# Self attention's group loop written out and folded, its scales made by a power on GpSimd, and the mixture's selector product moved behind the up product

## The chip, the cores and the metric

The kernel runs on one core of one Trainium2 chip. A core has five engines with a queue of their own each: TensorE (PE in the profile), VectorE (DVE), ScalarE (ACT), GpSimd (POOL) and SyncE (SP, which here only issues DMAs). An engine works its queue strictly in order; engines meet through semaphores alone. The metric is the device time of one execution in microseconds; lower is better.

## The reference, cut to what matters

The input `x` has 16 batch elements of 128 tokens with 128 features, the context 16 times 77 tokens. Four steps are added to `x`, each with a gate `tanh(g)` in front and a layer norm of `x` as its input:

```
x = x + tanh(g_xattn[0]) * strided_attention(layernorm(x), ctx, ctx)   # stage A: 16 heads, head h sees keys h, h+16, h+32, h+48
x = x + tanh(g_ffn[0])   * block(layernorm(x))                         # stage B: full self attention, then a mixture of 8 experts + shared
x = x + tanh(g_xattn[1]) * similarity_attention(layernorm(x), ctx)     # stage C, inside the mixtures
x = x + tanh(g_ffn[1])   * mixture(layernorm(x))                       # 16 experts + shared
```

Stage A, for one batch element: `Q = xn Wq^T + bq`, `K = ctx Wk^T + bk`, `V = ctx Wv^T + bv`, scores of each head over its 4 keys divided by sqrt(8), softmax over the 4, times `V`, then `Wo` and `bo`. Stage B begins with a layer norm followed by an RMS norm, and both need the mean and the variance of every row of `x` after stage A.

## The kernel before

The work is written out by hand for each engine in `build`; the order of the calls is the order of each queue, and there is no planner.

Stage A works through 4 groups of 4 batch elements. On DVE `norm` (line 757) makes the normalised tokens of a group, PE turns them over (`turn_and_project`, line 1235), ACT copies them out of PSUM (line 509), and PE multiplies them with Wq (line 1239, 512 columns) and the context with Wk and Wv (lines 1241 and 1242, 256 columns each). DVE adds the biases and masks keys and values by head (lines 786 and 789), PE multiplies the values by Wo (line 1248), and DVE adds `bo` (line 799). `strided_scores` (line 1256), DVE's maximum and subtraction (806, 808), ACT's exponential (513), DVE's sum, reciprocal and product (813 to 815), `turn_probabilities` (1263), ACT's copy (516), `attend` (1273), and DVE's update of `X` with new row statistics (`attended`, lines 823 and 827) close the group. Groups 0 to 2 run in a hardware loop (`Fori`) of all three engines, with one buffer of each kind; PE passes the next group's projections between scores and probabilities of this one. GpSimd has no part in the loop.

After group 3, DVE computes in a chain of single small instructions the moments of all 16 batch elements and the two inverse square roots (lines 744 to 861; a shift of bits as first guess and three Newton steps). Only then may GpSimd begin stage B.

Stage B goes batch element by batch element. GpSimd's `slot` makes in turn: the splitting of keys (lines 399 to 401), the normalised input `Z` of a later element (394), the splitting of queries (406 to 409), and `halves_of_weights` (420, 421), two pieces of the first mixture's weights. PE turns keys and queries over (line 1334), and works scores, values and denominators (1301 to 1328). All of it is staggered over slots: PE's `slot(of)` works on six elements at once.

Then follow the router and, from 218 us on, the two mixtures with stage C spread among them, in 112 chunks of 512 tokens (`chunks`). In a chunk PE makes the gate product in three passes (lines 1453 to 1455), at the first chunk of an expert the selector product `bc` (line 1498), which spreads the tokens' weights of this expert over all partitions into one PSUM bank, then the up product, then the down product of the chunk three before. ACT makes the silu (632) and a rounded copy (625), DVE multiplies silu by `bc` (1062) and by up (1067), and GpSimd subtracts the rounded copy (461).

## Time and profile before

| what | value |
|---|---|
| median of 3 runs | 563.38 us (563.04 to 566.1) |
| the profiled execution | 563.62 us, its span 561.9 us |
| mean granted TensorE clock | 0.929 of full speed |
| busy in the span | PE 467.4, DVE 403.4, ACT 265.8, POOL 257.3 us |
| first `Z` of stage B on GpSimd | at 66.97 us |
| first chunk of the mixtures on PE | at 218.00 us |

Times are microseconds from the start of the span; "ns" is said where meant. "PE L1453" is a matmul of line 1453. In a view of one stretch, `[1.59 <-DVE work L1062]` says that the engine had been idle for 1.59 us just before this instruction, and what its wait ended with. `x4` is the number of instructions in a row. One float32 matmul of the program appears as two in the trace. What lies outside the span, 1.7 us in the profiled execution, belongs to its time.

### The profile page before, as it was taken

The page shows a single profiled execution, that of the slowest core. Times are in us where ns is not written, and L with a number is a line of the kernel's source. Part 1 is how long each engine was busy: PE and PEld are TensorE (multiplying, and loading weights), DVE is VectorE, ACT ScalarE, POOL GpSimd, SP SyncE. Part 2 cuts the span into 40 slices and gives each one's busy share as a digit, 9 for nine tenths or more (in the row PEclk, how much of TensorE's full clock was granted, in tenths as well). Part 3 has the DMA queues.
Part 4 walks back from the last instruction along what each step waited for, and adds up shares of the span by engine and source line. Part 5 has one row for each costly group of instructions (what it writes and reads, how often), then busy time and mean ns, then how long its engine had stood idle before and what let it go on. Part 6 is the DMA issues. An engine that isn't in the chain of part 4 may idle for free.

```text
span 561.9 us, 10894 instructions
## 1 busy us (share of the span) xinstructions
PE 467.4 (83%) x3679; PEld 349.4 (62%) x3679; DVE 403.4 (72%) x1051; ACT 265.8 (47%) x494; POOL 257.3 (46%) x363
## 2 busy tenths in 40 slices
PE   2576279999999466999979988999798989798896
PEld 2344147676667354777757776768576766576674
DVE  6567568888987644895775677777877787677763
ACT  0211057777776234655536533644355346443452
POOL 6000079988960030555554544345445444343453
PEclk9878589999999855999989997999899999998999
DMA  6500000201010000200000000000000000000000
GB/s 163 173 0 0 0 3 2 85 23 51 3 34 19 1 0 0 48 0 1 1 2 0 2 1 2 1 0 0 0 0 1 0 1 1 20 0 21 0 20 19
DMA packets 19325, 9.79 MB, mean 17 GB/s; under 512 B 6508, under 2 KB 18765, under 8 KB 19277
## 3 DMA queue, kind: packets, MB, share of 16 engines
q1 hardware_dynamic: 16829, 8.77, 5.5%
q10 hardware_dynamic: 2448, 0.40, 0.4%
q8 instruction: 27, 0.44, 0.4%
q14 instruction: 21, 0.17, 0.1%
HBM read 8.12 MB, written 1.05 MB: 16 GB/s over the span
## 4 chain that ended last, share of the span: by engine, by line
PE 60%; DVE 18%; issue 8%; POOL 5%; ACT 5%; ACTq 2%; DVEq 1%; POOLq 0%
PE PS L1453 11%; PE PS L1455 10%; PE PS L1454 10%; DVE work L1062 3%; PE PS L1334 3%; PE PS L1323 3%; PE PS L1498 3%; PE PS L1328 2%; PE PS L1368 2%; PE PS L1301 2%; PE PS L1417 2%; PE PS L1239 1%; PE PS L1312 1%; DVE t_b L736 1%; POOL W0L_gate L421 1%
## 5 line engine op out<-in xcount | busy, mean ns | idle before, releaser
L461 POOL TENSOR_TENSOR HLO<-work,HHI 128x512 fp32r<-128x512 f32 x112 | 145.1, 1296 | 185.9 <-ACT HHI L625 185.4
L632 ACT ACTIVATE work<-PS 128x512 f32<-128x512 f32 x112 | 66.8, 597 | 110.1 <-PE PS L1455 106.3
L1062 DVE TENSOR_TENSOR work<-work,PS 128x512 f32<-128x512 f32 x104 | 71.0, 683 | 55.1 <-ACT work L632 53.5
L625 ACT ACTIVATE HHI<-work 128x512 fp32r<-128x512 f32 x111 | 69.5, 626 | 40.2 <-DVE work L1067 40.1
L1067 DVE TENSOR_TENSOR work<-PS,work 128x512 f32<-128x512 f32 x112 | 77.1, 691 | 12.1 <-PE PS L1455 3.4
L1498 PE MATMUL PS<-CWT,sel 128*128 128x512 bf16 (+1 forms) x68 | 27.2, 400 | 24.0 <-DVE work L1062 24.0
L870 DVE TENSOR_REDUCE nmax<-PS 128x4 f32<-128x512 f32 x64 | 42.2, 682 | 6.4 <-PE PS L1301 6.2
L531 ACT ACTIVATE EX<-PS 128x512 f32<-128x512 f32 x64 | 35.2, 605 | 13.3 <-PE PS L1312 13.2
L1453 PE MATMUL PS<-H2H,W0H_up 128*128 128x512 f32 (+1 forms) x72 | 36.8, 512 | 2.9 <-DVE work L1067 2.9
L1453 PE MATMUL PS<-H2H,W0H_gate 128*128 128x512 f32 (+1 forms) x72 | 32.7, 454 | 2.2 <-issue 1.5
L1498 PEld LDWEIGHTS PS<-CWT,sel 128*128 128x128 bf16 x68 | 6.6, 97 | 44.8 <-DVE work L1062 30.0
L394 POOL TENSOR_SCALAR Z<-X,rs,nmr 128x128 f32<-128x128 f32 x16 | 7.2, 449 | 56.1 <-DVE nmr L859 56.1
L1455 PE MATMUL PS<-H2H,W0L_up 128*128 128x512 f32 (+1 forms) x72 | 29.7, 413 | 0.0
L1454 PE MATMUL PS<-H2L,W0H_up 128*128 128x512 f32 (+1 forms) x72 | 29.7, 412 | 0.0
L1454 PE MATMUL PS<-H2L,W0H_gate 128*128 128x512 f32 (+1 forms) x72 | 29.4, 408 | 0.0
L1455 PE MATMUL PS<-H2H,W0L_gate 128*128 128x512 f32 (+1 forms) x72 | 29.3, 407 | 0.0
L1453 PE MATMUL PS<-HHI,W0H_down 128*128 128x512 f32 x72 | 29.2, 405 | 0.0
L1455 PE MATMUL PS<-HHI,W0L_down 128*128 128x512 f32 x72 | 29.1, 405 | 0.0
L1454 PE MATMUL PS<-HLO,W0H_down 128*128 128x512 f32 x72 | 29.1, 404 | 0.0
L549 ACT ACTIVATE QM<-PS 128x1024 bf16<-128x1024 bf16 x16 | 16.4, 1023 | 13.6 <-PE PS L1334 13.6
L1453 PE MATMUL PS<-H2H,W1H_up 128*128 128x512 f32 x40 | 22.5, 561 | 0.0
L1301 PE MATMUL PS<-KT,QT 64*128 64x128 bf16 x256 | 19.6, 218 | 1.7 <-DVE nmax L870 1.1
(290 smaller groups left out, 1174.7 us busy)
## 6 DMA issues: line engine op xcount, KB each, us to landing
X<-in_x_dram SPq DMA_DIRECT2D x4, 256.0 KB, 8.1
raw<-in_L_ffn_e_gate_dram SPq DMA_DIRECT2D x1, 1024.0 KB, 5.4
raw<-in_L_ffn_e_up_dram SPq DMA_DIRECT2D x1, 1024.0 KB, 7.7
out_dram<-X SPq DMA_DIRECT2D x4, 256.0 KB, 2.3
ctx_nat<-in_ctx_dram SPq DMA_DIRECT2D x1, 616.0 KB
raw<-in_L_ffn_We_gate_dram SPq DMA_DIRECT2D x1, 512.0 KB, 4.0
raw<-in_L_ffn_We_up_dram SPq DMA_DIRECT2D x1, 512.0 KB, 3.9
raw<-in_L_ffn_We_down_dram SPq DMA_DIRECT2D x1, 512.0 KB, 4.1
```

Source lines behind the costliest of these rows:

```text
L461: pool.tensor_tensor(HLO[t][:], HH[k % 2][:], HHI[t][:].bitcast(F32), ALU.subtract).then_inc(m_sem["lo"], 1)
L531: act.activation(EX[j][:], PS[:, 2 + j % 2, :], ACT.Exp, scale=SCALE).then_inc(b_sem["exp"], 1)
L625: act.activation(HHI[turn_of(m, g, k)][:], HH[k % 2][:], ACT.Copy).then_inc(S["hi"], 1)
L632: act.activation(SG[c % 2][:], PS[:, c % 2, :], ACT.Silu).then_inc(S["silu"], 1)
L870: dve.tensor_reduce(by_group[:, 4 * (j // 2):4 * (j // 2) + 4, j % 2], PS[:, j % 2, :].rearrange("p (h t) -> p h t", h=4), AX.X, ALU.max, ...
L1062: dve.tensor_tensor(SG[c % 2][:], SG[c % 2][:], PS[:, 4, :], ALU.mult).then_inc(S["scaled"], 1)
L1067: dve.tensor_tensor(HH[c % 2][:], PS[:, 2 + c % 2, :], SG[c % 2][:], ALU.mult).then_inc(S["hid"], 1)
L1301: ins = pe.matmul(PS[:, j % 2, i * P:(i + 1) * P], QT[b % 2][of_head, h // 2, :], KT[b % NKT][of_head, h // 2, :], start=True, stop=True)
L1453: pe.matmul(PS[:, bank, :], high, x_high, start=start, stop=False)
L1454: pe.matmul(PS[:, bank, :], high, x_low, start=False, stop=False)
L1455: return pe.matmul(PS[:, bank, :], low, x_high, start=False, stop=stop)
L1498: pe.matmul(PS[:, 4, :], SEL[m][:, e, :], CWT[:, bass.ds(g * GT, GT)], start=True, stop=True).then_inc(S["bc"], 1)
```

## The change

Stage A:

- The loop is written out for the four groups, and most buffers are doubled: normalised tokens (`XGA`), their transpose (`XGTA`), probabilities (`PA`, `PAT`), keys and values (`KA4`, `VA4`, in the memory of stage B's `QT` and `QM`).
- The query projection goes. Wq is multiplied into the masked keys (`fold_keys`: `KQ = Wq^T K`, 256 columns a group) and the scores are `xn KQ`; the bias bq enters through one more product with a broadcast tile `BQ` (`strided_scores`).
- GpSimd makes the normalised tokens (`normalised_group`) and adds `tanh(g) * bo` to `X` (`bias_group`). ACT, not DVE, copies the folded keys and values out of PSUM.
- GpSimd also makes the scales: of groups 1 to 3 of the first norm (`first_scales`), and of stage B's norms in two halves of 8 batch elements (`scales_of_half`), by an elementwise power -0.5 and one Newton step. DVE keeps the scales of group 0.
- The last group's end is put among stage B's first slots: on DVE `probabilities(3)` and `attended(3)`, on PE `turn_probabilities(3)` and `attend(3)`, on ACT the copies between them.
- Seven small transfers move from ACT's queue to SP's, ahead of stage B's weights; the context comes in two halves, each with a semaphore.

Mixtures: on PE the selector product stands behind the up product. In a chunk the wait for DVE's `scaled` of the chunk before stands there too.

```diff
@@ stage A's tiles
+            XGA, XGTA = [XG, HG1], [XGT, work[0]]
+            KA4, VA4 = ([t[u][:]... for u in range(2)] for t in (QT, QM))
+            KQ = [EX[g][:, 0:GB * NK].rearrange("p (b k) -> p b k", b=GB) for g in range(G)]
@@ GpSimd
+            def moments(at, n):
+                st = stats[:, at, :]
+                pool.tensor_tensor(p_a[:, 0:n], st[:, :, 1], st[:, :, 4], ALU.add)
...
+                step(pool.tensor_tensor(var[:, at], p_b[:, 0:n], p_c[:, 0:n], ALU.add))
+            def inverse_root(y, v, t):
+                step(pool.tensor_tensor(y, v, less_half[:].broadcast_to([P, v.shape[1]]), ALU.pow))
+                step(pool.tensor_tensor(t, y, y, ALU.mult))
+                step(pool.tensor_tensor(t, t, v, ALU.mult))
+                step(pool.tensor_scalar(t, t, -0.5, 1.5, ALU.mult, ALU.add))
+                step(pool.tensor_tensor(y, y, t, ALU.mult))
+            def scales_of_half(k):
+                pool.wait_ge(a_sem["st"], 2 * k + 2)
+                moments(at, HALF)
...
+            normalised_group(0)
+            pool.tensor_copy(BQ[:], bq_c[:].broadcast_to([P, P])).then_inc(a_sem["bq"], 1)
+            first_scales(1, G)
+            normalised_group(1)
...
-            batches(slot, 0, 3)
+            scales_of_half(0)
+            batches(slot, -3, 1)
+            scales_of_half(1)
+            batches(slot, 1, B)
@@ DVE
-            with dve.Fori(0, G - 1) as g:
-                norm(g + 1)
-                less_row_maximum(g)
-                probabilities(g)
-                queries_keys_values(g + 1)
-                attended(g)
-                values_out(g + 1)
...
+            masked_keys_values(0)
+            masked_keys_values(1)
+            less_row_maximum(0)
+            masked_keys_values(2)
+            probabilities(0)
+            less_row_maximum(1)
+            masked_keys_values(3)
+            attended(0)
+            probabilities(1)
+            less_row_maximum(2)
+            attended(1)
+            probabilities(2)
+            less_row_maximum(3)
+            attended(2)
@@ DVE, start of stage B
-            batches(slot, 0, 6)
+            queries_and_keys(0)
+            values_apart(0)
+            probabilities(3)
+            queries_and_keys(1)
+            values_apart(1)
+            turned_keys(0)
+            attended(3)
+            queries_and_keys(2)
+            batches(slot, -3, -1)
...
@@ PE, mixtures
                     split_product(c % 2, WH[m][0][:, c, :], WL[m][0][:, c, :], xh, xl).then_inc(S["g"], 1)
+                    if not (start and c < 2):
+                        pe.wait_ge(S["hid"], base + c)
+                    split_product(2 + c % 2, WH[m][1][:, c, :], WL[m][1][:, c, :], xh, xl).then_inc(S["u"], 1)
                     if first_of_expert(m, c):
                         e = c // per
                         pe.wait_ge(S["scaled"], g * NSC[m] + OFF[m][1] + e * per + 1)
                         pe.matmul(PS[:, 4, :], SEL[m][:, e, :], CWT[:, bass.ds(g * GT, GT)], start=True, stop=True).then_inc(S["bc"], 1)
-                    if not (start and c < 2):
-                        pe.wait_ge(S["hid"], base + c)
-                    split_product(2 + c % 2, WH[m][1][:, c, :], WL[m][1][:, c, :], xh, xl).then_inc(S["u"], 1)
```

PE in stage A, before: the body of the loop, for one group (`ctx_t` is the turned context, `VA` the masked values, `PA` the probabilities).

```order
L1256 MATMUL PS<-KA,work 128x64 x4
L1232 REGISTER_ALU
L1235 MATMUL PS<-identf,XG 128x128 x4
L1239 MATMUL PS<-XGT,w_t 128x512
L1241 ISA
L1241 MATMUL PS<-ctx_t,w_t 128x256
L1242 MATMUL PS<-ctx_t,w_t 128x256
L1263 MATMUL PS<-identf,PA 128x128 x2
L1273 MATMUL PS<-work 128x128 x4
L1248 MATMUL PS<-w_t,VA 128x128 x2
```

PE now, from the scores of group 1 on (`QT` holds the masked keys, `QM` the masked values, `EX` the folded keys, `E3T` the folded values).

```order
L1368 MATMUL PS<-QT,BQ 128x256
L1370 MATMUL PS<-EX,work 128x64 x4
L1343 MATMUL PS<-QT,w_nat 128x256
L1336 MATMUL PS<-ctx_t,w_t 128x256
L1337 MATMUL PS<-ctx_t,w_t 128x256
L1348 MATMUL PS<-w_t,QM 128x128 x2
L1379 MATMUL PS<-identf,work 128x128 x2
L1393 MATMUL PS<-E3T,work 128x128 x4
L1357 MATMUL PS<-identf,XG 128x128 x4
```

The 512 columns of the query projection are gone; 256 columns of the fold and 256 of the bias stand for them, and the context's products of group 3 come before group 0 is closed.

GpSimd at the start of stage B, before: from the last of its constants on.

```order
L361 MEMSET bm 4x1
L394 TENSOR_SCALAR Z<-X,rs,nmr 128x128 x2
L399 TENSOR_TENSOR T<-T,KS 128x128
L400 CAST KS<-T 128x32x8
L401 TENSOR_TENSOR KS<-T,KS 128x16x8
```

GpSimd now, second place: the end of the last weight piece of element 0, and the first rows of the second half's scales (18 instructions; the same 18 stand ahead of the first `Z`, too).

```order
L513 TENSOR_TENSOR W0L_gate<-raw0,W0H_gate 128x256
L385 TENSOR_TENSOR p_a<-stats 128x8
L386 TENSOR_TENSOR p_b<-stats 128x8
L387 TENSOR_TENSOR p_c<-stats 128x8
L388 TENSOR_SCALAR mean<-p_a 128x8
L389 TENSOR_SCALAR p_c<-p_c 128x8
L390 TENSOR_TENSOR p_b<-p_b 128x8
L391 TENSOR_SCALAR p_b<-p_b 128x8
```

Work of DVE has moved to GpSimd, into the row of its slots between elements 0 and 1.

## Rows read from the trace of the kernel before

**Rows 1.** Busy time in stretches: span, PE, PEld, DVE, ACT, POOL, clock, DMA

```profile
30.00:50.00 20.00, 13.55 (x65) 8.94 (x64) 14.07 (x38) 2.57 (x6) 0.00 (x0) 0.84 0.00 0
...
105.00:172.00 67.00, 66.60 (x1237) 46.77 (x1238) 58.31 (x129) 49.68 (x88) 54.16 (x123) 1.00 0.16 44
218.00:562.00 344.00, 308.87 (x1467) 236.80 (x1467) 247.99 (x587) 166.96 (x319) 158.58 (x132) 0.97 0.02 6
```

**Rows 2.** The chain that ended last, in stage A: start us, us, what

```profile
36.50 0.68 PE PS L1235 x4
37.28 0.61 ACT XGT L509
37.93 1.82 PE PS L1239 x2
39.75 0.85 PE PS L1241 x2
...
42.38 0.74 PE PS L1273 x8
...
46.66 0.68 PE PS L1235 x4
```

**Rows 3.** Timeline of the start, all engines: start us, us, instruction, idle before

```profile
8.97 2.26 PE L1226 MATMUL PS<-identf,ctx_nat 77*128 77x77 f32 x16
...
11.22 2.67 DVE L766 BATCH_NORM_STATS2 stats<-X 128x6 f32<-128x128 f32 x12
11.30 0.46 ACTq L495 DMA_DIRECT2D bqv_r<-in_L_xattn_b_qv_dram  x1
...
12.81 1.28 ACT L499 ACT_TABLE_LOAD   x1 [12.81 <-issue]
```

**Rows 4.** DVE's groups of instructions in 35.3 to 45.5: busy, mean ns

```profile
L827 DVE BATCH_NORM_STATS2 stats<-X x4 | 0.9, 282 | 0.1
L786 DVE TENSOR_SCALAR work<-PS,bq_c 128x512 f32<-128x512 f32 x1 | 0.8, 750 | 1.7 <-PE PS L1242 1.7
L813 DVE TENSOR_REDUCE mxA<-PA 128x64 f32<-128x256 f32 x1 | 0.6, 583 | 1.0 <-ACT PA L513 1.0
L814 DVE RECIPROCAL mxA<-mxA 128x64 f32<-128x64 f32 x1 | 0.6, 553 | 0.0
L789 DVE SCALAR_TENSOR_TENSOR KA<-PS,bk_c,hmask 128x256 f32<-128x256 f32 x1 | 0.5, 475 | 0.0
...
L815 DVE TENSOR_TENSOR PA<-PA,mxA 128x256 f32<-128x256 f32 x1 | 0.4, 424 | 0.0
```

**Rows 5.** Timeline at the end of stage A

```profile
62.73 0.18 DVE L744 TENSOR_TENSOR t_a<-stats 128x16 f32<-128x16 f32 x1
...
66.97 0.88 POOL L394 TENSOR_SCALAR Z<-X,rs,nmr 128x128 f32<-128x128 f32 x2 [56.14 <-DVE nmr L859]
```

**Rows 6.** GpSimd's groups by shape, 66 to 172

```profile
L394 POOL TENSOR_SCALAR Z<-X,rs,nmr 128x128 f32<-128x128 f32 x16 | 7.2, 449 | 56.1 <-DVE nmr L859 56.1
...
L369 POOL CAST iota_e<-iota_i 128x16 f32<-128x16 int32 x1 | 0.2, 196 | 0.1
```

**Rows 7.** The page's group of GpSimd's widest operation

```profile
L461 POOL TENSOR_TENSOR HLO<-work,HHI 128x512 fp32r<-128x512 f32 x112 | 145.1, 1296 | 185.9 <-ACT HHI L625 185.4
```

**Rows 8.** The chain that ended last, in stage B

```profile
81.14 0.40 POOL T L399
...
105.33 0.62 PE PS L1334 x8
```

**Rows 9.** Who waited for whom in 200 to 540: total us, times, longest

```profile
PE PS L1498 <- DVE work L1062: 24.0, 11, 4.0
```

**Rows 10.** Timeline of the mixtures, one undisturbed chunk, then the first stall

```profile
228.64 0.39 PE L1498 MATMUL PS<-CWT,sel 128*128 128x512 bf16 x1
...
229.47 0.69 DVE L1062 TENSOR_TENSOR work<-work,PS 128x512 f32<-128x512 f32 x1
...
284.54 0.61 PE L1498 MATMUL PS<-CWT,sel 128*128 128x512 bf16 x1 [3.56 <-DVE work L1062]
```

More of the change, by code:

```diff
@@ L263, in batches @@
         def batches(slot_of, first, last):
-            for s in range(-last, B - first):
+            for s in range(first, last):
                 slot_of(lambda k: s + k if 0 <= s + k < B else None)
@@ L276, in _, with tokens, context @@
         def _(sp):
[L278 removed]
+            def tokens(g):
                 sp.dma_start(X[:, g * GB:(g + 1) * GB, :], a["x"][g * GB:(g + 1) * GB].rearrange("b s d -> s b d")).then_inc(x_in[g], 16)
[L280 to L281 removed]
+            def context(k):
+                at = slice(k * B // 2, (k + 1) * B // 2)
+                sp.dma_start(ctx_nat[:, at, :], a["ctx_1024"][at].rearrange("b s d -> s b d")).then_inc(ctx_in[k], 16)
+            tokens(0)
+            context(0)
+            context(1)
+            for g in range(1, G):
+                tokens(g)
+            smalls = [(n1w[:], col(a["L0_ffn_norm1_w"])), (n2w[:], col(a["L0_ffn_norm2_w"])),
+                      (w1_c[:], col(a["L1_xattn_w_sim"][0:D])), (w2s[:], col(a["L1_xattn_w_sim"][D:2 * D])),
+                      (w3s[:], col(a["L1_xattn_w_sim"][2 * D:3 * D])), (bsim_c[:], row(a["L1_xattn_b_sim"], P)),
+                      (bqv_r[:], row(a["L1_xattn_b_qv"], P))]
+            for to, what in smalls:
+                sp.dma_start(to, what).then_inc(small_in, 16)
             for i, n in enumerate(("wq", "wk")):
@@ new lines, in normalised_group, with bias_group @@
+            def normalised_group(g):
+                if g == 0:
+                    pool.wait_ge(a_sem["ln"], 1)
+                if g >= 2:
+                    pool.wait_ge(a_sem["t"], g - 1)
+                for j in range(GB):
+                    b = g * GB + j
+                    ins = pool.tensor_scalar(XGA[g % 2][:, j, :], X[:, b, :], rstd[:, b:b + 1], nmr[:, b:b + 1], ALU.mult, ALU.add)
+                ins.then_inc(a_sem["xn"], 1)
+            def bias_group(g):
+                pool.wait_ge(a_sem["xn"], g + 1)
+                Xg = X[:, g * GB:(g + 1) * GB, :]
+                pool.tensor_tensor(Xg, Xg, tgbo[:].unsqueeze(1).broadcast_to([P, GB, D]), ALU.add).then_inc(a_sem["bias"], 1)
@@ new lines, in _ @@
+            normalised_group(0)
+            pool.wait_ge(bias_in, 16 * 3)
+            pool.tensor_copy(BQ[:], bq_c[:].broadcast_to([P, P])).then_inc(a_sem["bq"], 1)
+            first_scales(1, G)
+            normalised_group(1)
+            pool.wait_ge(tg_ready, 1)
+            pool.wait_ge(bo_in, 16)
+            step(pool.tensor_scalar(tgbo[:], bo_r[:], tg[:, 0:1], None, ALU.mult))
+            bias_group(0)
+            bias_group(1)
+            for g in range(2, G):
+                normalised_group(g)
+                bias_group(g)
@@ new lines, in masked_keys_values @@
+            def masked_keys_values(g):
+                if g == 0:
+                    dve.wait_ge(bias_in, 16 * 3)
+                    dve.wait_ge(consts, 1)
+                dve.wait_ge(a_sem["kv"], g + 1)
+                if g >= 2:
+                    dve.wait_ge(a_sem["s"], g - 1)
+                    dve.wait_ge(a_sem["v2"], g - 1)
+                mask = hmask[:].unsqueeze(1).broadcast_to([P, GB * L, H])
+                for to, off, bias in ((KA4[g % 2], 0, bk_c), (VA4[g % 2], GB * NK, bv_c)):
+                    ins = dve.scalar_tensor_tensor(
+                        out=to.rearrange("p b (l h) -> p (b l) h", h=H),
+                        in0=PS[:, 5 + g % 2, off:off + GB * NK].rearrange("p (a h) -> p a h", h=H),
+                        scalar=bias[:], in1=mask, op0=ALU.add, op1=ALU.mult)
+                ins.then_inc(a_sem["kv_sb"], 1)
@@ L826, in attended @@
+            def attended(g):
+                dve.wait_ge(a_sem["y"], g + 1)
+                dve.wait_ge(a_sem["bias"], g + 1)
+                Xg = X[:, g * GB:(g + 1) * GB, :]
+                dve.scalar_tensor_tensor(out=Xg, in0=PS[:, 1, :].rearrange("p (b d) -> p b d", b=GB),
+                                         scalar=tg[:, 0:1], in1=Xg, op0=ALU.mult, op1=ALU.add).then_inc(a_sem["x"], 1)
+                dve.wait_ge(a_sem["x"], g + 1)
                 for j in range(GB):
                     ins = dve.bn_stats(stats[:, g * GB + j, :], X[:, g * GB + j, :])
-                ins.then_inc(a_sem["x"], 1)
@@ new lines, in fold_keys, with fold_values @@
+            def fold_keys(g):
+                pe.wait_ge(a_sem["kv_sb"], g + 1)
+                if g >= 1:
+                    pe.wait_ge(a_sem["v2_sb"], g)
+                pe.matmul(PS[:, 0, 0:GB * NK], w_nat[:, 3, :], KA4[g % 2], start=True, stop=True).then_inc(a_sem["kq"], 1)
+            def fold_values(g):
+                pe.wait_ge(a_sem["kq_sb"], g + 1)
+                for k in range(2):
+                    ins = pe.matmul(PS[:, 0, k * D:(k + 1) * D], VA4[g % 2][:, 2 * k:2 * k + 2, :].rearrange("p b k -> p (b k)"), w_t[:, 2, :],
```

371 lines of the change are left out of this document (202 added, 169 removed).

## The prediction, made before the changed kernel was run

> **What bounds the kernel now.** I read the busy time by stretches first, then the chain that ended last, then the timelines of its weak places. There are three regimes. In stage A no engine is full: in 30 to 50 us PE is busy 13.55 and DVE 14.07 of 20 us [rows 1], and the chain passes from PE to ACT to PE, and by way of DVE to the next group: one pass of the loop, from turning one group to turning the next, takes 46.66 - 36.50 = 10.16 us [rows 2]. Stage A then ends with a serial chain of small instructions on DVE, and GpSimd gets its first `Z` at 66.97 [rows 5]. In stage B the chain runs on GpSimd until 105.33, where PE turns queries that GpSimd has just split, and after that on PE, which is busy 66.60 of 67 us [rows 8, 1]. So what comes earlier or later before 105.33 moves all that follows; what GpSimd is given in this stretch costs its full price. In the mixtures PE is busy 308.87 of 344 us, and the largest single wait of PE is that of the selector product for DVE: 24.0 us in 11 places [rows 1, 9].
>
> **The first `Z` in the changed kernel.** I walk the new queues with the old durations.
>
> *Start.* ACT loads its table only at 12.81, behind the issues of the seven small transfers, the last at 11.30 [rows 3]. At about half a microsecond to over one for each, some 4 us, these now stand in SP's queue ahead of stage B's weights, which nobody wants before stage B. ACT's copies of weights and context are then done when PE has turned the context, at 11.2 [rows 3], and the first keys and values are made from 11.2 to 12.9 (2 x 0.85 [rows 2]). DVE no longer normalises group 0, but its statistics of groups 1 to 3 need the last tokens, which may not have landed when it first could take them; they ended at 11.22 + 2.67 = 13.9 [rows 3], and I take 13.4.
>
> *Groups.* Costs, all from [rows 2, 4]: keys and values 1.7, fold of keys 0.85, fold of values about 0.7 (as 256 columns or a little under), turning 0.68, scores 0.85 for the bias product and 1.0 to 1.1 for the four narrow ones, so 1.95; turning probabilities half of 0.68 and latency, 0.5; attending 0.74 and the new wait between its halves, 0.9. PE's sum is 7.4 us a group. ACT: 0.6 for a copy of 512 columns and 0.4 for one of 256. DVE: masking 2 x 0.475, maximum and subtraction 2 x 0.42, probabilities 0.58 + 0.55 + 0.42 = 1.56, update 0.75 and statistics 4 x 0.22 to 0.28, about 1.65: 5.0 us a group. A hop between engines is 0.1.
> From 13.4: masking 14.3, fold 15.2, keys and values of group 1 to 17.0, fold of values 17.7, turning 18.5, ACT's copy 19.3, scores(0) 21.3. Then PE goes on (fold, keys and values of group 2, fold of values, turning: 3.95) to 25.3; ACT first copies values and does the exponential of group 0, so tokens are there at 26.2 and scores(1) end at 28.2. Fold, products of group 3, fold of values: 31.5. Turning probabilities(0) 32.0, ACT 32.5, attend(0) 33.5, DVE's update 35.3 and probabilities(1) 36.9, turning 37.5, scores(2) 39.4, attend(1) 40.3, `attended(1)` with its statistics 42.1. At this moment `scales_of_half(0)` may start. PE meanwhile goes on to attend(2), about 47.
>
> *Scales.* The DVE chain took 66.97 - 62.73 = 4.24 us for 20 instructions [rows 5], 0.21 each. GpSimd has 18, of which 13 wait for the one before. Its conversion of 16 columns took 0.196 us [rows 6]; its widest operation takes 1.296 us for 512 columns [rows 7] and the normalisation 0.449 for 128 [rows 6], which makes 2.2 ns a column and 0.17 us for none. I take 0.21 for each: 3.8 us. **The power** is in no row. As cheap as a product it costs 0.2 us for 16 columns; upwards, twenty times the 2.2 ns a column would be 0.7, and I let it go to 3. I take 1.0, nearer to the product, since only 16 columns are asked for. So 4.8 us, and the first `Z` at 42.1 + 0.1 + 4.8 = 47.0 instead of 66.97: **-20.0**. Bounds: if the walk is that of PE alone (11.2 + 4 x 7.4 less what stands behind group 1), 43; if a hop more is lost at every step, 53.
> The Trainium skill, "GPSIMD Engine Reference", section "Engine selection", says to do elementwise work on VectorE because GpSimd needs about twice as long with two inputs. The rows above show that at 8 to 16 columns the fixed part decides and the two are alike. By the rule the 18 instructions would take some 7.4 us twice, the sum would be 5 us worse, 552; no run here shows GpSimd at this width with two inputs.
> The other users of GpSimd are hidden: `first_scales(1, G)` follows four normalisations (1.8) and ends near 17, its tokens of group 1 are ready near 19 and PE turns them at 24.6, so the power has 5 us of room there. The bias adds (4 x 1.3 [rows 7]) and two more groups end before 30.
>
> **Start of stage B: +1.1.** DVE has `probabilities(3)` (1.56) and `attended(3)` (1.65) in front of projections of elements 1 and 2, and PE turns probabilities(3) before it projects element 1. That holds up the queries of element 1, on which GpSimd waits before its first weight pieces, by 1.0 to 1.2. The 1.65 of `attended(3)` hits element 2, which GpSimd takes up later than that.
>
> **Second half of the scales: +4.8.** It stands in GpSimd's queue between the weight pieces of element 0 and `split_keys(2)`, the row at 81.14 [rows 8], in the stretch where the chain is GpSimd's. Nothing hides it. Queued behind are the splittings of elements 2 to 5, and PE waits for them. It needs the statistics of group 3, which DVE has some 12.5 us after the first `Z`, and GpSimd comes to it after 15: no wait. Range 3.8 to 7. After 105.33 PE needs 6.8 us an element (the stretch's 67 us hold ten) and GpSimd less, so nothing is caught up or lost.
>
> **Mixtures: -3.** In an undisturbed chunk the selector product starts at 228.64 and DVE multiplies at 229.47 [rows 10], as soon as the silu is there. Behind the up product it starts three passes of 0.23 later, ends at 229.7, and DVE begins about 0.3 later. PE is not held by that. Where DVE is behind, as at 284.54 with 3.56 us of idle [rows 10], PE now does the up product (0.69 us) inside the wait, since its own condition is older. The 11 waits are seven separate episodes as I read the timeline (some follow directly on another, and a second one gives nothing more): 7 x 0.69 = 4.8, less 0.3 for the later start of DVE in the four of the second mixture, less some 0.2 in three places where the up product itself waited. Bounds +3 to -6.
>
> **Sum.** 563.62 - 20.0 + 1.1 + 4.8 - 3.0 = 546.5. The profiled execution is 0.24 above the median, which I leave. Own range of this case: 541 to 552.
>
> **The rivals.**
> *The power is slow (slower than before).* If GpSimd computes it lane by lane, X us instead of 1, both halves pay, and `first_scales` pays what is over 6. Speaks for it: no row shows a power, and the operation needs a logarithm and an exponential. Against: the dearest row costs 2.5 ns a column. The gain of 17 is gone at X near 8.6; with X = 10 the sum is 546.5 + 18 + 4 = 568.5. Chance 0.05.
> *The selector product behind the up product costs.* If the 0.3 us of later start add up at each of the DVE-bound places rather than being taken up by the 0.7 us and more that DVE has free in a chunk (247.99 busy of 344 [rows 1]), the mixtures are 3 slower, not faster: 552.5. Chance 0.13.
> *The group order does not flow.* Each engine's queue is fixed; if one is badly placed (ACT's exponential behind the values' copy of the next group, DVE's masking of group 3 in front of the update), a group keeps costing near the old 10 us for two of them and the first `Z` comes at 53 to 54: 553. For it: my walk already has PE idle for 6 us between its products. Chance 0.17.
> *More is won.* PE alone sets stage A (first `Z` at 43), the power is as cheap as a product: 546.5 - 4 - 1.6, 541 or less. Chance 0.2.
> The forecast itself 0.45.
>
> **Chances.** 0.5% is 2.8 us, about what a measurement of this kernel tells from no change. Slower by more holds the slow power, 0.04; within, 0.03, between it and the order that does not flow; faster 0.93. The range 538 to 558 leaves out the slow power, the far end of the badly flowing order and the best of the fast case, some 0.17.
>
> **What would show it.** First `Z` on GpSimd at 45 to 49 (53 would be the third rival). The power as a row of GpSimd (128 x 16) of 1 us; over 5 would be the first rival. From the first `Z` to the point where the chain leaves GpSimd for PE: 38.4 us before, 44.3 now. PE's wait in front of the selector product falls from 24.0 to about 19, and the time from the first mixture chunk to the end from 344 to 341; if it grows, the second rival is right. A first `Z` over 60, or a chain in stage B that waits on DVE instead, would make the prediction wrong.

## The result, and the profile after

The changed kernel takes 545.5 us (median of 4 executions, 544.9 to 546.3), the kernel before beside it 563.2. The ratio is 0.9675, 95% interval 0.9641 to 0.9709. The forecast was 546.5 (538 to 558). In a second measurement, on another occasion, it was 546.2 us (5 executions, 545.4 to 546.3) beside 564.6, ratio 0.9668 (0.9644 to 0.9691). The profiled execution took 544.93 us, with a span of 542.4. Of all executions told below one, at 549.21 us of the kernel without the Newton step, counts as slow (over 1.5% above the fastest of the same kernel) and is left out of that kernel's figures.

In the changed program the gate, up and down products stand in lines 1600 to 1602, the selector product in 1648, its use on DVE in 1164, the power in 396, `Z` in 486, and the last step of the splitting of queries in 501. I cut the span at five points: the first `Z`, the split queries of elements 1, 2 and 5 (`q1`, `q2`, `q5`: the start of GpSimd's last step on them), and the first gate product of the mixtures.

| stretch | before | after | difference | forecast |
|---|---|---|---|---|
| start to first `Z` | 66.97 | 44.20 | -22.8 | -20.0 |
| `Z` to `q1` | 11.46 | 12.33 | +0.9 | +1.1 |
| `q1` to `q2` | 5.54 | 13.00 | +7.5 | +4.8 |
| `q2` to `q5` | 20.87 | 21.35 | +0.5 | 0 |
| `q5` to the first gate product | 113.16 | 113.36 | +0.2 | 0 |
| mixtures to the end of the span | 343.9 | 338.2 | -5.7 | -3.0 |
| span | 561.9 | 542.4 | -19.5 | -17.1 |

Outside the span the profiled execution has 2.5 us, 0.8 more than before. The busy times by stretches, with the columns of [rows 1]:

```profile
9.00:30.00 21.00, 16.74 (x98) 13.64 (x97) 11.68 (x36) 7.33 (x19) 17.52 (x37) 1.00 0.55 146
30.00:50.00 20.00, 12.38 (x53) 8.95 (x53) 10.08 (x25) 4.25 (x10) 12.39 (x33) 0.67 0.00 1
50.00:70.00 20.00, 13.71 (x103) 8.76 (x102) 10.62 (x23) 7.81 (x14) 16.28 (x45) 0.76 0.01 1
70.00:172.00 102.00, 100.38 (x1854) 70.86 (x1858) 83.96 (x185) 73.75 (x127) 73.01 (x165) 0.98 0.11 30
204.00:542.00 338.00, 307.54 (x1467) 235.24 (x1467) 246.49 (x587) 167.48 (x320) 158.94 (x132) 0.97 0.02 6
```

The first row has PE busy 80% of the time; in the kernel before it was 58% in the same stretch (12.16 of 21 us) and two thirds in [rows 1]. In the mixtures PE's busy time is nearly as before (307.5 against 308.9), and the stretch is 5.7 us shorter: most of the gain there is idle time of PE. From 30 to 70 us the granted clock is low (0.67 and 0.76), which matters below.

The chain that ended last, from the input's landing to the point where it leaves GpSimd for PE for the last time (it takes the place of [rows 2, 5, 8]; start us, us, what):

```profile
4.50 7.77 DMA X<-in_x_dram
12.30 0.88 DVE stats L882 x4
...
15.61 2.31 POOL rstd L396
...
35.52 0.88 DVE stats L933 x4
...
39.26 2.94 POOL rs L396
...
61.79 2.93 POOL rs L396
...
70.02 1.03 PE PS L1476 x8
```

The power stands in it three times, 8.2 us together. The new statistics of the first half end at 36.4, where the walk had 42.1. GpSimd's timeline from there to the first `Z` (start us, us, instruction, out<-in; in full 18 instructions, and the same 18 again from 59.21 to `split_keys(2)` at 66.70):

```profile
36.47 0.21 POOL L385 TENSOR_TENSOR p_a<-stats 128x8 f32<-128x8 f32 x1 [2.65 <-DVE stats L933]
...
38.66 0.24 POOL L414 TENSOR_SCALAR var<-var 128x8 f32<-128x8 f32 x1
38.97 0.20 POOL L415 TENSOR_SCALAR var<-var 128x8 f32<-128x8 f32 x1
39.26 2.93 POOL L396 TENSOR_TENSOR rs<-var,less_half 128x16 f32<-128x16 f32 x1
42.26 0.21 POOL L397 TENSOR_TENSOR p_d<-rs 128x16 f32<-128x16 f32 x1
42.56 0.22 POOL L398 TENSOR_TENSOR p_d<-p_d,var 128x16 f32<-128x16 f32 x1
...
44.20 0.88 POOL L486 TENSOR_SCALAR Z<-X,rs,nmr 128x128 f32<-128x128 f32 x2
```

The power of 16 columns takes 2.93 us, its neighbours 0.20 to 0.24. Read the starts too: an instruction that needs the one before follows it after 0.29 to 0.31 us, not after its own 0.21. So the chain takes 7.7 us instead of the 4.8 of the forecast, and 7.5 us the second time.

PE's wait before the selector product, in 175 to 530 (total us, times, longest), and the stall that answers to the one in [rows 10]:

```profile
PE PS L1648 <- DVE work L1164: 18.8, 9, 3.2
```

```profile
270.11 0.39 PE L1648 MATMUL PS<-CWT,sel 128*128 128x512 bf16 x1 [2.86 <-DVE work L1164]
```

24.0 us in 11 places became 18.8 in 9, and the stall of 3.56 became 2.86: 0.70 less, the up product's three passes. Each of the other long ones (3.96, 3.95, 3.24 before) is shorter by the same 0.7 to 0.8; one that follows directly on another is not (2.66 before, 2.69 now), as the forecast had it.

### The profile page after: what moved, and what is told of

Read it like the earlier page. It is cut to its first block, busy times and chain, and to the rows that moved or that the text cites. A ratio compares the mean times of both kernels' runs of the same rounds, so it can differ in the third digit from the quotient of the medians.

```text
span 542.4 us, 10818 instructions
## 1 busy us (share of the span) xinstructions
PE 465.7 (86%) x3686; PEld 351.2 (65%) x3686; DVE 384.5 (71%) x983; ACT 269.2 (50%) x502; POOL 289.1 (53%) x437
## 4 chain that ended last, share of the span: by engine, by line
PE 61%; DVE 19%; issue 7%; POOL 6%; ACT 4%; DMA 1%; SPq 1%; POOLq 0%; DVEq 0%; ACTq 0%
PE PS L1600 10%; PE PS L1601 9%; PE PS L1602 9%; PE PS L1476 4%; DVE work L1164 4%; PE PS L1465 3%; PE PS L1470 3%; PE PS L1510 3%; PE PS L1438 3%; PE PS L1648 2%; PE PS L1453 2%; PE PS L1564 2%; DMA X<-in_x_dram 1%; DVE work L1169 1%; DVE t_b L855 1%
## 5 line engine op out<-in xcount | busy, mean ns | idle before, releaser
L1164 DVE TENSOR_TENSOR work<-work,PS 128x512 f32<-128x512 f32 x104 | 71.0, 683 | 56.8 <-PE PS L1648 37.8
L960 DVE TENSOR_REDUCE nmax<-PS 128x4 f32<-128x512 f32 x64 | 42.3, 683 | 8.4 <-PE PS L1438 8.3
L1648 PE MATMUL PS<-CWT,sel 128*128 128x512 bf16 (+1 forms) x68 | 27.0, 397 | 18.8 <-DVE work L1164 18.8
L646 ACT ACTIVATE EX<-PS 128x512 f32<-128x512 f32 x64 | 35.2, 605 | 13.4 <-PE PS L1453 13.4
L1600 PE MATMUL PS<-HHI,W0H_down 128*128 128x512 f32 x72 | 35.1, 487 | 0.0
L1600 PE MATMUL PS<-H2H,W0H_up 128*128 128x512 f32 (+1 forms) x72 | 30.0, 417 | 2.9 <-DVE work L1169 2.9
L1600 PE MATMUL PS<-HHI,W1H_down 128*128 128x512 f32 x40 | 22.4, 560 | 1.1 <-POOL HLO L556 1.1
L1438 PEld LDWEIGHTS PS<-KT,QT 64*128 64x128 bf16 x256 | 11.8, 97 | 15.5 <-issue 10.3
```

The source lines that it names most:

```text
L646: act.activation(EX[j][:], PS[:, 2 + j % 2, :], ACT.Exp, scale=SCALE).then_inc(b_sem["exp"], 1)
L960: dve.tensor_reduce(by_group[:, 4 * (j // 2):4 * (j // 2) + 4, j % 2], PS[:, j % 2, :].rearrange("p (h t) -> p h t", h=4), AX.X, ALU.max, ...
L1164: dve.tensor_tensor(SG[c % 2][:], SG[c % 2][:], PS[:, 4, :], ALU.mult).then_inc(S["scaled"], 1)
L1438: ins = pe.matmul(PS[:, j % 2, i * P:(i + 1) * P], QT[b % 2][of_head, h // 2, :], KT[b % NKT][of_head, h // 2, :], start=True, stop=True)
L1600: pe.matmul(PS[:, bank, :], high, x_high, start=start, stop=False)
L1648: pe.matmul(PS[:, 4, :], SEL[m][:, e, :], CWT[:, bass.ds(g * GT, GT)], start=True, stop=True).then_inc(S["bc"], 1)
```

## The experiments

All were run beside the kernel before; its median in the four measurements was 563.2 to 564.8 us. The theory after the first look: the forecast's terms are right in kind, the power costs 2.9 us each time it stands in the chain, and the selector product's new place gives all of the mixtures' gain.

### The selector product alone, in both directions

```
+                    if not (start and c < 2):
+                        pe.wait_ge(S["hid"], base + c)
+                    split_product(2 + c % 2, WH[m][1][:, c, :], WL[m][1][:, c, :], xh, xl).then_inc(S["u"], 1)
                     if first_of_expert(m, c):
                         e = c // per
                         pe.wait_ge(S["scaled"], g * NSC[m] + OFF[m][1] + e * per + 1)
                         pe.matmul(PS[:, 4, :], SEL[m][:, e, :], CWT[:, bass.ds(g * GT, GT)], start=True, stop=True).then_inc(S["bc"], 1)
-                    if not (start and c < 2):
-                        pe.wait_ge(S["hid"], base + c)
-                    split_product(2 + c % 2, WH[m][1][:, c, :], WL[m][1][:, c, :], xh, xl).then_inc(S["u"], 1)
```

> The kernel before with the one edit of the mixtures alone: the selector product behind the up product. Theory (each wait of the selector product is shortened by the up product's 0.69 us, and DVE's later start costs nothing): the mixtures from PE's first chunk to the end 338.2 us as in the changed kernel, against 343.9 before, so 557.6 us in all, -5.7. Rival 1, the bookkeeping of the prediction (DVE's later start costs 0.3 in four places): -3, 560.4. Rival 2, the gain of the mixtures in the changed kernel came from elsewhere (a different state of buffers or clock at their start): no change, 563.

Measured: 557.38 us (556.99 to 558.03), beside 564.77 for the kernel before, ratio 0.987 (0.9846 to 0.9894). From PE's first chunk of the mixtures to the end it is 338.6 us instead of 343.9. The other direction, the changed kernel with the selector product back in front:

> The changed kernel with the selector product in its old place, so stage A and the start of stage B alone. Theory (the two parts are independent and add up): 545.5 + 5.7 = 551.2 us, and the first mixture chunk of PE at 204.2 as in the changed kernel. Rival: they share a gain, and it is 548 or 545.

Measured: 551.75 (551.01 to 556.39), ratio 0.977 (0.9748 to 0.9791). PE's wait of the two, first of the kernel before with the move, then of the changed kernel without it:

```profile
PE PS L1501 <- DVE work L1062: 18.6, 9, 3.2
```

```profile
PE PS L1645 <- DVE work L1164: 23.5, 9, 4.0
```

The wait follows the place of the product, whatever stage A does, and the time follows the wait. With the move the kernel before is 7.4 us faster than its neighbour of the same measurement, and 5.9 us faster than the 563.2 of the first measurement, which is the kernel that the expectation started from; without it the changed kernel is 5.5 to 6.2 us slower than its two medians. The profile's 5.3 and the wait's 5.4 us lie nearer to the lower figures. The two parts of the change add up within the noise: the two ratios multiply to 0.964, and the whole change has 0.9675 (0.9641 to 0.9709). The rival of the forecast that DVE's later start costs is gone, although DVE's product with the selector's output now waits for PE: 37.8 us in 33 places in 175 to 545, where it had no such wait before; its wait for ACT's silu fell from 50.0 to 17.4.

### The power

```
-                step(pool.tensor_tensor(y, v, less_half[:].broadcast_to([P, v.shape[1]]), ALU.pow))
+                step(pool.tensor_tensor(y, v, less_half[:].broadcast_to([P, v.shape[1]]), ALU.mult))
```

This kernel leaves out the inverse roots: a product stands in the power's place.

> The changed kernel in which GpSimd's power is a multiplication of the same operands; the inverse square roots of groups 1 to 3 and of stage B are left out of the computation by it. The power took 2.30, 2.93 and 2.92 us, a product takes 0.21. Theory (only part of the first two is on the path: PE waited 0.44 us for the tokens of group 1, and in front of the first Z PE and DVE are busy with group 2 until 1.3 us before it; the third is on it in full): 0.44 + 1.3 + 2.7 = 4.4 us faster, 541. Rival (all three in full): 7.5 us faster, 538. Rival (the second half's scales are hidden since PE is the bound from 70 us on): 1.7 us faster, 543.8.

Measured: 540.89 (538.84 to 542.93), ratio 0.9577 (0.9549 to 0.9604). The row of the power in the changed kernel and here:

```profile
40.06 0.22 POOL L396 TENSOR_TENSOR rs<-var,less_half 128x16 f32<-128x16 f32 x1
```

0.22 us instead of 2.93. The power costs about 5 us of the kernel. Against the second measurement of the changed kernel, whose start is alike, the first `Z` comes 3.0 us earlier (42.30 against 45.27) and `q1` to `q2` is 2.8 shorter (10.25 against 13.01), while `Z` to `q1` is 1.4 longer. The power of `first_scales` (2.30 us for 12 columns) was to have 5 us of room. It had less, since PE comes to the tokens of group 1 at 20.8 instead of 24.6, but PE waits only this for them:

```profile
21.27 0.66 PE L1357 MATMUL PS<-identf,HG 128*128 128x128 f32 x4 [0.44 <-POOL HG L428]
```

The next one keeps the power and drops the Newton step behind it, 4 instructions in each of its three uses:

```
                 step(pool.tensor_tensor(y, v, less_half[:].broadcast_to([P, v.shape[1]]), ALU.pow))
-                step(pool.tensor_tensor(t, y, y, ALU.mult))
-                step(pool.tensor_tensor(t, t, v, ALU.mult))
-                step(pool.tensor_scalar(t, t, -0.5, 1.5, ALU.mult, ALU.add))
-                step(pool.tensor_tensor(y, y, t, ALU.mult))
```

> The changed kernel without the Newton step after the power, so four small instructions of 0.29 us less in each of the three places; it also tells how exact the power is. Theory: 1.1 us in the second half's scales in full, 1.1 before the first Z, 0.4 at group 1: 2 to 2.5 us faster, 543.

Measured: 543.09 (538.19 to 545.56, five executions), ratio 0.9616 (0.9575 to 0.9657). The median is 2.4 to 3.1 us under the changed kernel's two. The profiled execution, against the changed kernel's with a like start, has a span 2.2 us shorter (0.9 up to the first `Z`, 1.3 in `q1` to `q2`), as 2 x 4 x 0.3 us would have it. The spread of 7.4 us is larger than that, and comes below.

### The second half's scales elsewhere

In the changed kernel they stand in the middle of GpSimd's stretch of the chain. First, on VectorE in four pieces of 5 or 6 instructions between its slots, with the seed and three Newton steps of the kernel before (the first three lines are in GpSimd's program, which then waits for the last piece before `Z` of element 8):

```
-            batches(slot, -3, 1)
-            scales_of_half(1)
-            batches(slot, 1, B)
+            batches(slot, -3, B)
...
-            batches(slot, -3, -1)
+            batches(slot, -3, -2)
+            second_half(0, 6)
+            batches(slot, -2, -1)
...
-            batches(slot, -1, B)
+            second_half(6, 11)
+            batches(slot, -1, 0)
+            second_half(11, 16)
+            batches(slot, 0, 1)
+            second_half(16, 21)
+            batches(slot, 1, B)
```

> The changed kernel with the scales of batch elements 8 to 15 made by DVE in four pieces of five or six small instructions each between its slots (shift of bits and three Newton steps, 21 instructions of 0.2 us), and nothing of them on GpSimd. Theory (GpSimd's 7.5 us between the weight pieces of element 0 and the keys of element 2 are on the path in full, and DVE has room): 7 us faster than the changed kernel, 538.5; GpSimd hands over the queries of element 2 at about 62.5 instead of 69.95. Rival (PE bounds stage B from 70 us on and would not come sooner by more than its own start): 0 to 2 us faster. Rival (DVE's 4.4 us now hold up the projections): 3 us faster.

Measured: 545.56 (540.97 to 547.7), ratio 0.9647 (0.9612 to 0.9682): no gain, where 7 us were expected. Next, left on GpSimd but four elements later:

```
-            batches(slot, -3, 1)
+            batches(slot, -3, 5)
             scales_of_half(1)
-            batches(slot, 1, B)
+            batches(slot, 5, B)
```

> The changed kernel with GpSimd's scales of the second half behind its slot of element 4, that is just ahead of the normalisation of element 8, which needs them. Theory (GpSimd never has 7.5 us of slack before element 8, so the wait only moves from element 2 to element 6): within 1 us of the changed kernel, 545. Rival (PE is the bound from 70 us on, so GpSimd's queue has room later): 6 us faster, 539.5.

Measured: 549.68 (546.97 to 552.19), ratio 0.9735 (0.9708 to 0.9763): slower than the changed kernel, against both expectations. The stretches of the profiled executions tell why (the changed kernel here is that of its second measurement, which has the same start as the other two, see below):

| us | `Z` | to `q2` | `q2` to `q5` | `q5` to `q7` | to gate | mixtures |
|---|---|---|---|---|---|---|
| changed kernel, again | 45.27 | 25.34 | 21.36 | 11.87 | 101.50 | 338.2 |
| pieces on VectorE | 45.47 | 19.73 | 25.42 | 13.37 | 101.86 | 338.3 |
| late on GpSimd | 45.52 | 19.84 | 22.03 | 18.50 | 103.42 | 339.5 |

Both have the 5.5 us where they were looked for, up to `q2`. The pieces give 4.1 of them back up to `q5` and 1.5 behind it, after the last piece (90.0 us), which is not explained; the late scales give back 0.7, and then pay 6.6 where they stand, and 3 more behind. So an early `q2` is not lost by itself (22.03 against 21.36); what eats it is the work on VectorE. The chain that ended last shows it. In the kernel with the pieces it passes through them; this is the third, with the row maximum (`nmax`) that stands behind it and the products of PE that wait for that:

```profile
81.02 0.09 DVE rs L1042
...
81.34 0.31 DVE t_d L1041
...
81.89 0.28 DVE t_d L1040
...
82.19 0.70 DVE nmax L961
...
82.94 0.39 PE PS L1474 x4
```

In 73.9 to 104 us the instructions of the pieces have 3.3 us of this chain. In the changed kernel it is on PE alone there. The busy time between `q3` and `q7`, with the pieces:

```profile
73.90:104.00 30.10, 27.96 (x520) 19.60 (x521) 27.63 (x68) 20.52 (x37) 22.94 (x52) 1.00 0.20 51
```

and of the changed kernel between its own `q3` and `q7`:

```profile
76.50:102.80 26.30, 26.30 (x495) 18.56 (x488) 23.48 (x52) 19.55 (x36) 22.92 (x52) 1.00 0.22 58
```

PE is full there in the changed kernel, 26.3 of 26.3 us, and VectorE looks as if it had 2.8 us to spare. With the pieces VectorE is busy 27.6 of 30.1 us, 4.1 more (3.3 of it are the pieces that fall there), and PE has 2.1 us of idle time: the 2.8 us were gaps between steps that others wait for, and work put into the queue there delays the next step. The same holds for GpSimd, whose queue at the late place is as much part of the ring as at the early one. There (waits in 86 to 112):

```profile
PE PS L1476 <- POOL KS L493: 4.5, 1, 4.5
```

### Is it the clock? Throwaway products on TensorE

In the changed kernel the granted clock falls to 0.50 behind PE's wait of 2.69 us that ends at 37.97, and stays low, with interruptions, until 75 us. The cheapest explanation for the gain that the pieces did not bring was that the start of stage B runs at half clock anyway. Five products before the probabilities of group 2, two behind its values, and one and one behind:

```
+            def filler(n):
+                for _ in range(n):
+                    pe.matmul(PS[:, 5, 0:GB * NK], w_t[:, 0, :], ctx_t[:, 0:GB, 0:NK], start=True, stop=True)
...
             turn_group(3)
+            filler(5)
             turn_probabilities(2)
```

> The changed kernel with nine idle products on PE (256 columns, result unused) in places where PE waits in its trace: five before it turns the probabilities of group 2 (idle 2.69 us there), two before the first input of stage B, one on either side of the input of element 1. In the changed kernel the granted clock is 1.00 until 36 us and 0.50 from 39 to 54. Theory (what the wait at 35 us loses is the clock, and PE's pieces of the chain from 44.8 to 54, some 6 us at the low level, would take half): clock 1.00 on from 36 us, 2 to 4 us faster than the changed kernel, 542.5. Rival (the clock falls all the same, and the idle products only stand in the way): 1 us slower, 546.5.

> The scales of the second half on DVE in pieces, together with the same nine idle products. Alone, the pieces gave nothing (545.6): GpSimd handed over the queries of element 2 at 65.2 instead of 69.5, but the granted clock stayed at 0.50 until 70 us and elements 3 and 4 came 8.7 and 8.3 us apart. Theory (the gain was lost to PE's low clock): with the clock up, 540. Rival (it was lost to DVE's 4.4 us more work between the row maxima, which the clock doesn't change): 543 to 545.

Measured: 546.84 (545.36 to 551.05), ratio 0.9695 (0.9666 to 0.9723), and with the pieces 543.55 (542.61 to 548.37), ratio 0.9644 (0.9615 to 0.9673). Both came out as the rival of their expectation, not as its theory (542.5 and 540). The profiled execution with the products alone says little of the clock: its products came to full speed late (see below), and its clock was at 0.50 from 38 to 44 us, before the five products, with PE busy 5.94 of 6 us. In the one with the pieces the clock stood at 1.00 until 42 us instead of 36, then fell all the same in the next gap, and was at 0.50 in 57 to 74 although PE was busy 93% of the time:

```profile
57.00:74.00 17.00, 15.84 (x141) 10.37 (x142) 11.83 (x32) 8.53 (x14) 12.48 (x31) 0.50 0.01 2
```

So the products were made many (6, 12, 4 and 4, and 12, 8 and 5 narrow ones before the third block of scores of elements 0, 1 and 2), beside the changed kernel itself:

```
             turn_group(3)
+            filler(6)
             turn_probabilities(2)
...
             attend(2)
+            filler(12)
...
                 if of(3) is not None:
+                    if of(3) < 3:
+                        filler_7((12, 8, 5)[of(3)])
                     scores(of(3), 2)
```

> The changed kernel once more, beside the next three on the same chip, to see how far single executions of it spread. The four executions at hand lie between 544.9 and 546.3 us; the variants with the same start spread over up to 11 us. If the spread belongs to the start (how long TensorE's granted clock stays at half in 36 to 76 us), the median is 545.5 and single ones may lie 4 us away.

> The changed kernel with throwaway products in every gap of TensorE between the last turned group and element 2 of the self attention: 6 products of 256 columns before the third group's probabilities, 12 behind its values, 4 and 4 behind the first projection and the second turned input, and 12, 8 and 5 of 104 columns before the third block of scores of elements 0, 1 and 2. Theory (the granted clock is what keeps the start from being shorter; it stays high only while TensorE has work): the clock stays at 1.00 from 36 us until the wait for the second half's scales, and the time is 543 (541 to 544.5). Rival (the ring of GpSimd, TensorE and VectorE sets the pace there, whatever the clock): 545.5 or more, the products only cost.

> The second half's scales in pieces on VectorE, and the same throwaway products as in the run before. In the run with few of these products the clock fell at 44 us and again at 57, and TensorE was busy at half clock from 57 to 74. Theory of the clock: held at 1.00 over that stretch, elements 2 and 3 are handed over at 61 and 67 us instead of 62.2 and 70.9, and the time is 538 (535.5 to 541). Rival: the ring sets the pace, 543.5 as with few products.

> As the run before, and the first half's inverse root is the power alone, without its Newton step (4 small instructions of about 0.3 us less on GpSimd ahead of the first normalised input). Theory: 1.2 us less than the run before, 537. It is the version meant to beat both kernels. If the time follows the granted clock more than the work, it lies within the spread of the run before.

Measured: the changed kernel 546.23 (above); with many products 547.69 (546.54 to 550.98), ratio 0.969 (0.9665 to 0.9714); with pieces and products 544.89 (542.92 to 550.78), ratio 0.9681 (0.9634 to 0.9728); the same without the Newton step 544.35 (543.43 to 550.42), ratio 0.9669 (0.963 to 0.9707). Busy times of the pieces with many products, and, in the second fence, of the changed kernel:

```profile
34.00:44.00 10.00, 9.82 (x55) 8.06 (x55) 6.40 (x17) 1.81 (x4) 5.90 (x15) 1.00 0.00 0
44.00:57.00 13.00, 12.05 (x67) 9.02 (x65) 4.21 (x9) 4.16 (x9) 6.83 (x20) 1.00 0.01 2
57.00:74.00 17.00, 16.11 (x205) 12.66 (x208) 13.98 (x39) 9.06 (x15) 13.46 (x34) 1.00 0.00 1
```

```profile
34.00:44.00 10.00, 6.78 (x28) 5.53 (x28) 4.57 (x12) 1.81 (x4) 6.55 (x18) 0.65 0.00 0
44.00:57.00 13.00, 9.28 (x43) 5.28 (x43) 6.38 (x18) 4.27 (x9) 7.03 (x20) 0.62 0.00 1
57.00:74.00 17.00, 11.15 (x94) 6.93 (x94) 9.34 (x20) 7.62 (x13) 15.20 (x39) 0.71 0.00 1
```

The products did what they were to do, the clock is 1.00 throughout, and the time hardly moved. They stand in the queue themselves. The chain of the same kernel:

```profile
41.89 5.44 PE PS L1435 x24
47.33 0.12 PE PS L1552
...
57.55 2.85 PE PS L1439 x24
60.41 0.33 PE PS L1484 x4
```

`Z` is there at 45.02 and is turned only at 47.33, because PE is still busy with nothing. From `Z` to `q2` it took 20.13 us, 0.4 more than with the pieces at half clock. From `q2` to `q7` it took 36.67 against 38.79, and against 33.23 in the changed kernel: about 2 of the pieces' loss may be put down to the clock; more than 3 is there at full clock too (the products in the way are part of it, as far as they delay the chain there). Over the whole way from `Z` to `q7` it is 58.6 us in the changed kernel, 58.5 with the pieces, 57.8 with pieces and few products, 56.8 with pieces and many, and 60.5 with many products alone. Whether fewer products at better places would keep the clock and delay nothing was not tried. My expectation of 538 was wrong, and so were those of 537 for the same without the Newton step and of 543 for the changed kernel with products alone, where the rival held.

None of the variants stands clearly ahead of the changed kernel: the best medians, 543.1 (no Newton step), 543.6 (pieces and few products) and 544.4 (all together), are 1.2 to 3.1 us under its two, and the intervals of their ratios overlap with its own, that of the kernel without the Newton step only just (0.9575 to 0.9657 against 0.9644 to 0.9691), in another measurement. The kernel with a product for the power is faster, but it leaves out the inverse roots.

### Where the spread comes from

Single executions of one variant lay up to 8 us apart (542.92 to 550.78 with pieces and many products). The profiled ones show one cause: a pair of products of 256 columns in stage A takes 0.85 us up to some moment and 0.44 from then on, and the moment differs. The first fast pair starts at 14.3 us in the changed kernel and at 13.9 with pieces and few products, at 19 to 20 in the changed kernel's second measurement and in seven variants, and at 27.8 and 28.4 in two (few products alone, and the selector product back in front). From the chain of the variant with few products alone, whose profiled execution took 551.05 us:

```profile
21.02 1.60 PE PS L1370 x8
...
23.58 0.85 PE PS L1336 x2
...
28.44 0.84 PE PS L1370 x8
...
29.77 0.44 PE PS L1336 x2
```

The first `Z` follows: 44.20 and 44.09 where the moment was near 14, 45.0 to 45.5 (46.2 with many products) where it was near 19, 49.9 and 50.9 where it was near 28. Only the kernels that have less to do in front of it come sooner at a moment near 19: 44.4 and 44.0 without the Newton step, 42.3 with a product for the power. From `q7` to the first gate product it is 101.5 to 101.9 us in all of them but the late one. So a comparison of two profiled executions means something only where this moment is the same, as in the table above. It is not the whole spread: the profiled execution with many products alone, 550.98 us, had it near 20, and lost 1.8 us in `q2` to `q5` and 2.7 in the mixtures; why is open.

## Why the prediction was right, point by point

*Time and sum.* 546.5 was forecast, 545.5 and 546.2 measured. The sum is close because three terms were off by 2.7 to 2.8 us and not all on one side: -2.8 in stage A, +2.7 for the second half's scales, -2.7 in the mixtures; with -0.2 in `Z` to `q1`, +0.7 behind `q2` and +0.8 outside the span the profiled execution ends 1.6 under the sum. The terms have the right sign and kind; that the sum is this close is partly luck. Of the signs that were named, PE's wait came as named (18.8 for about 19), the first `Z` at 44.2 lies just outside 45 to 49, and the power's row was 2.9 us, not 1.

*First `Z`: right in kind, mis-sized in two places that partly cancelled.* The start held: keys from 11.13, last statistics at 13.17 (13.4 forecast, and they did wait for the tokens, 0.95 us). The step that failed is "2 x 0.85" for keys and values, with 0.85 for the folds and 1.95 for scores. These prices were read from a stretch of the kernel before in which the clock was at half: in [rows 1] it is 0.84 on average over 20 us, but around the product at 39.75 [rows 2] it was this, in the kernel before:

```profile
39.00:42.00 3.00, 2.82 (x7) 1.50 (x6) 1.31 (x3) 0.06 (x1) 0.00 (x0) 0.56 0.00 0
```

In the new order PE runs denser and the same pair took 0.44. The walk's 7.4 us a group became about 5, and the statistics of group 1 ended at 36.4 instead of 42.1, -5.7. Against it stand the scales, 7.7 instead of 4.8 us, +2.9. The two executions in which the pair kept its 0.85 us until 28 us bear this out: there the statistics of group 1 are complete at 42.1 and 43.1, as in the walk. GpSimd's first instruction behind them, first with the selector product back in front, then with few products:

```profile
42.16 0.21 POOL L385 TENSOR_TENSOR p_a<-stats 128x8 f32<-128x8 f32 x1 [8.09 <-DVE stats L933]
```

```profile
43.13 0.21 POOL L385 TENSOR_TENSOR p_a<-stats 128x8 f32<-128x8 f32 x1 [9.02 <-DVE stats L933]
```

*The scales.* The power at 1.0 us was the wrong choice between 0.2 and 3; it is 2.93, at the upper end. A power isn't priced like a product: 12 columns took 2.30 us and 16 took 2.93, by these two sizes 0.16 us a column, where the forecast read 0.0022 from the widest operation and the normalisation. And 0.21 us for each small instruction was the busy time; with the wait for the one before it is 0.29. GpSimd at this width with two inputs, which no row showed before, takes 0.20 to 0.22 us, against DVE's 0.18 [rows 5]. The rule of the Trainium skill ("GPSIMD Engine Reference", section "Engine selection") that GpSimd needs about twice as long there is not borne out at 8 to 16 columns, where it is some 1.2 times as long.

*Start of stage B:* +0.9 for +1.1. *Second half's scales:* nothing hid them, as forecast, and the experiment with the scales four elements later shows that nothing would hide them there either. Their 7.5 us stand whole in `q1` to `q2`.

*Mixtures.* The mechanism, the up product inside the wait, is shown in both directions. The size was off by the two deductions from 7 x 0.69 = 4.8: DVE's later start at 0.3 us in four places, and 0.2 in three more. The episodes themselves gave 5.2 by the timeline, and the later start cost nothing that can be seen. The other 0.5 us of the stretch's 5.7 are not assigned. The second rival (0.13) fell with it.

*Rivals.* The slow power got 0.05 for "over 5 us"; at 2.93 us it isn't that, but it eats 5 us: with a product in its place the kernel takes 540.9, which is the "541 or less" of "more is won". (By that rival's own terms, twice X - 1 and once X - 6, the gain of 17 us is gone at X near 8.4, not 8.6.) The group order flowed.

*Chain.* From the first `Z` to where it leaves GpSimd: 38.4 before, 44.3 forecast. Here the point itself moved, since it leaves at 70.02 (25.8 us after `Z`) instead of 105.33, and the split queries of one and the same element are the better mark: +8.3 for `q2` against +5.9.

## What to carry to other kernels

A price read from a stretch at low clock is a price at low clock: before a duration of TensorE is used for a denser order of work, look at the granted clock over the few microseconds of that very row, not over the stage, and at how long a known product took there, since the clock can read 1.00 over slow products all the same (below). Small operations on a slower engine cost their cadence, not their busy time, and the power on GpSimd cost by the column, so an operation that no row shows is to be measured before it is put on a chain. Idle time of an engine inside a ring that is full elsewhere isn't free: 21 small instructions, 4.9 us together, on a VectorE that was 89% busy (23.48 of 26.30 us) took back what moving them off GpSimd had gained, 5.6 us, about 2 of that by the low clock.

## What the runs showed of the hardware that was not expected

The power on GpSimd took 2.30 us for 128 x 12 and 2.93 us for 128 x 16 (float32); the same line as a product took 0.22 at 16 columns.

Products of TensorE ran at about half their speed in the first 14 to 28 us while the granted clock of the same windows read 1.00. The windows of the kernel with few products alone, around the pairs of 0.85 us at 23.58 and of 0.44 at 29.77 above:

```profile
21.00:24.00 3.00, 3.00 (x13) 2.73 (x12) 0.85 (x2) 0.38 (x1) 2.92 (x5) 1.00 0.83 249
...
27.00:30.00 3.00, 2.23 (x14) 2.13 (x15) 2.14 (x5) 0.80 (x2) 2.92 (x6) 1.00 0.59 194
```

The load of the DMA engines, 0.83 in the slow window, does not explain it: in the changed kernel it was 0.94 and 1.10 in 21 to 24 and 24 to 27, and the pair at 24.70 took 0.44. So the clock column does not show every slow stretch; the duration of a known product does. What makes these products slow is not shown. When it comes to the full speed differs by up to 14 us between executions of nearly the same instructions, and with it up to 6 us of this kernel's time.

The granted clock fell to 0.50 after PE had been idle 2.69 us, and stood at 1.00 over the same stretch (36 to 42 us) when five products filled that gap (pieces and few products). Such a gap is neither needed nor enough at once: with few products alone it fell near 38 us behind waits of 1.08 us at most, and with the selector product back in front it still read 1.00 in 42 to 44, over most of the same wait of 2.69 us, and 0.50 from 45 on, with PE busy. In 57 to 74 us it was 0.50 with PE busy 15.84 of 17 us (pieces and few products), so being busy again did not bring it back at once.
